# Input codes of a four-bit feed-forward: excess on ScalarE, total in place in PSUM, code difference on VectorE, product alone on GpSimd

## The chip, the cores and the metric

The kernel runs on one core of a Trainium2 chip. The metric is the device time in microseconds (us) of one execution. The engines are TensorE (PE), VectorE (DVE), ScalarE (ACT), GpSimd (POOL) and the DMA queues of SyncE (SP). They run side by side and meet at semaphores.

## The reference

Eight blocks in a row, each added to a residual stream x of shape (8, 512, 128): a selective scan, a feed-forward in four-bit codes, linear attention, the same feed-forward again, a forgetting attention, a linear map with signs, a rotary attention, and the linear map again. Only the two four-bit feed-forwards are touched, and in them only how the normalised input gets its codes:

```python
def _layernorm(x, axis=-1, eps=1e-05):
    m = jnp.mean(x, axis=axis, keepdims=True)
    v = jnp.var(x, axis=axis, keepdims=True)
    return (x - m) / jnp.sqrt(v + eps)

def fp4_quant_dequant(x):            # BLOCK = 16
    xb = x.reshape(shape[:-1] + (shape[-1] // BLOCK, BLOCK))
    scale = jnp.max(jnp.abs(xb), axis=-1, keepdims=True) / 6.0
    scale = jnp.maximum(scale, jnp.float32(1e-12))
    xn = xb / scale
    idx = jnp.searchsorted(_MID, jnp.abs(xn))
    q = _GRID[idx] * jnp.sign(xn) * scale
    return q.reshape(shape)

gate = fp4_linear(x, w_gate)         # fp4_linear: both operands through fp4_quant_dequant
y = fp4_linear(x, w_up)
h = jax.nn.silu(gate) * y
return fp4_linear(h, w_down)
```

The grid is 0, 0.5, 1, 1.5, 2, 3, 4, 6.

## The kernel before, in words

The kernel is a chain of stages. A stage opens its tiles and semaphores, writes out by hand what each engine does in order (one function per engine in a block), and ends with a barrier of all engines; nothing of the next stage starts before it. `ffn0_stages` holds two of them, `fx` (input codes) and `fh` (hidden layer), and is called twice, once for each four-bit feed-forward.

Stage `fx` works on 8 sequences of 512 tokens in PAIRS = 4 pairs. A pair is 8 tiles of 128 tokens by 128 channels, 1024 columns, in one of RING = 3 tiles of PSUM (`cps`, shown as fx_ps_c). Blocks of 16 channels lie next to each other, 64 blocks a pair.

- TensorE, `center(g)` (L728): 8 products with the centring matrix, 16 matmul instructions in the profile. g = 0 to 3 serves the moments and block maxima; g = 4 to 7 makes the same values again for the codes, since PSUM holds three pairs only. The last of them, center(7), writes the ring tile that pair 0 of the codes has used and so waits for it.
- ScalarE: squares with sums (L756), then logarithm and exponential for the inverse root (L772, L774).
- VectorE: block maxima (L787), the root's refinement (L794 to L801), then `codes` (L807 to L813) for all four pairs at once: normed, above (the scale, a hair larger), inv, both.
- Then for every pair k: VectorE `scaled` (L819) multiplies the tile in PSUM by both, so it holds xn. ScalarE `sizes` (L762) takes size = |xn| x 2^22. VectorE `total` takes mag = max(size, ROUND), ROUND = 1.5 x 2^22 (L824), and tot = mag + xn (L826): adding so large a number rounds xn to the grid. GpSimd takes q = tot - mag (L843) and xq = q x above (L846), 1024 columns each. TensorE `back` (L737) transposes the 8 tiles into two PSUM tiles, and ScalarE `out` (L767) copies them to XQ, which stage `fh` reads.

Most tiles behind the ring are double (index k % 2), and the waits on semaphores say when one is free again. The order on each engine is as written; VectorE goes scaled(0), then scaled(k+1), total(k).

Of the kernel before, what the change touches and what calls it, by code (L numbers as in the profile page):

```python
# [9 lines left out]
ALU = mybir.AluOpType  # L10
# [3 lines left out]
P = 128  # L14
# [6 lines left out]
FQ = 16  # L21
# [672 lines left out]
def ffn0_stages(nc, w, X):  # L694
# [7 lines left out]
    with Stage(nc, "ffn") as outer:  # L702
        XQ = outer.sb("xq", [P, B, T])
        with Stage(nc, "fx") as st:
# [8 lines left out]
            size, mag, tot, q, xq = ([st.sb(f"{n}{k}", [P, NB, FQ]) for k in range(2)] for n in ("size", "mag", "tot", "q", "xq"))  # L713
            s = st.sems("cent sq lnv rough var v1 v2 rstd amax normed above inv both xn size mag tot q xq back out")
            with st.block() as block:

                @block.tensor
                def _(pe):
                    def center(g):
                        k, before = g % PAIRS, g - RING  # L720
                        if before >= PAIRS:
                            pe.wait_ge(s.tot, before - PAIRS + 1)
                        elif before >= 0:
                            pe.wait_ge(s.sq, TOK * (before + 1))
                            pe.wait_ge(s.amax, before + 1)
# [22 lines left out]
                def _(act):  # L748
# [35 lines left out]
                def _(dve):  # L784
# [4 lines left out]
                    def tokens(t):  # L789
                        return t[:, :, :].rearrange("p k (t a) -> p (k t) a", t=TOK)  # L790
# [12 lines left out]
                    def codes():  # L803
                        r = widen(rstd[:, :, :].rearrange("p k t -> p (k t)"), XB)
                        dve.wait_ge(s.rstd, 1)
                        dve.wait_ge(s.amax, PAIRS)
                        dve.tensor_tensor(tokens(normed), tokens(amax), r, ALU.mult).then_inc(s.normed, 1)  # L807
                        dve.wait_ge(s.normed, 1)
                        dve.tensor_scalar(above[:, :, :], normed[:, :, :], ABOVE / 6.0, ABOVE * 1e-12, ALU.mult, ALU.max).then_inc(s.above, 1)
                        dve.wait_ge(s.above, 1)  # L810
                        dve.reciprocal(inv[:, :, :], above[:, :, :]).then_inc(s.inv, 1)
                        dve.wait_ge(s.inv, 1)
# [1600 lines left out]
```

## Time and profile before

| what | value |
|---|---|
| median of 3 runs | 2164.16 us (2164.16 to 2165.03) |
| the profiled execution | 2161.56 us |
| its span on the core | 2159.8 us |
| busy TensorE / VectorE / ScalarE / GpSimd | 85% / 78% / 65% / 49% |
| DMA | 39 GB/s mean |

The profile is of one execution; its times count from the span's start. A row of the order of time gives start, duration, engine, line, operation, the tiles out<-in, their sizes and a count; brackets hold the idle time of the engine ahead of it and what ended that. The granted TensorE clock is 1.00 for 2.4 GHz and 0.50 for 1.2 GHz. The two runs of stage `fx` begin near 381 and 629 us.

### The profile page before, as it was taken

Reading aid. Unit: us, or ns where it says so; the run is one execution under the profiler, and the core shown is the slowest. Engines: PE = TensorE matmul, PEld = TensorE weight load, DVE = VectorE, ACT = ScalarE, POOL = GpSimd, SP = SyncE. Lnnn points to the kernel's source line nnn. Section 1 sums busy time; section 2 is a strip of 40 time slices with the busy share of each in tenths; the row PEclk is TensorE's granted clock in tenths of the full one; section 3 lists DMA queues with packets and bytes.
Section 4 is the critical chain, followed back from the end, with each engine's and each line's share of the span. In section 5 each row is a group of like instructions: output and inputs, shape, how many; then the busy total and the mean of one; then the engine's idle time right before and its main releaser. Section 6 shows DMA issues by size and latency. Waiting matters only on the chain. (4 is left out here: it accounts for less than half of the span.)

```text
span 2159.8 us, 36543 instructions
## 1 busy us (share of the span) xinstructions
PE 1836.5 (85%) x12003; PEld 886.7 (41%) x12003; DVE 1680.9 (78%) x2274; ACT 1400.2 (65%) x2314; POOL 1056.2 (49%) x1121
## 2 busy tenths in 40 slices
PE   5558886687886857999999999999999967789997
PEld 2123332553664423555555555555554423222222
DVE  5979996596346958888888888888887636798884
ACT  3547774375335736777777777777776524689994
POOL 0167774364106714666666666666666521431112
PEclk9779998699997979999999999999999978999999
DMA  3000000000000011111111112221111100422210
GB/s 96 0 15 0 0 0 0 1 1 1 0 0 0 1 57 42 48 62 62 58 62 59 56 61 62 62 62 61 57 56 64 42 20 15 103 75 58 57 48 39
DMA packets 71432, 84.48 MB, mean 39 GB/s; under 512 B 20544, under 2 KB 44032, under 8 KB 71168
## 3 DMA queue, kind: packets, MB, share of 16 engines
q1 hardware_dynamic: 69536, 81.69, 12.5%
q8 instruction: 91, 1.49, 0.3%
q10 hardware_dynamic: 1728, 0.67, 0.1%
q14 instruction: 77, 0.63, 0.1%
HBM read 71.95 MB, written 9.57 MB: 38 GB/s over the span
## 5 line engine op out<-in xcount | busy, mean ns | idle before, releaser
L1761 DVE SCALAR_TENSOR_TENSOR fu_kv<-fu_ps_kv,fa_vec,fu_kv 128x511 f32<-128x511 f32 (+2 forms) x384 | 286.0, 746 | 56.3 <-ACT fu_kv L1633 51.1
L1844 POOL TENSOR_TENSOR fu_ds<-fu_p 128x768 f32<-128x768 f32 x64 | 115.8, 1810 | 188.7 <-PE fu_ps_ss L1532 188.5
L2199 ACT ACTIVATE rt_p<-rt_ps_s 128x1024 f32<-128x1024 f32 x192 | 185.6, 1029 | 25.1 <-PE rt_ps_s L2130 25.1
L1492 PE MATMUL fu_ps_s<-fu_qn,fu_kn 64*128 64x512 f32 (+3 forms) x1024 | 190.0, 468 | 1.4 <-DVE fu_sg L1722 0.7
L625 POOL TENSOR_TENSOR scan_hC<-scan_h,scan_c 128x1024 f32<-128x1024 f32 x64 | 150.9, 2357 | 71.7 <-DVE scan_h L601 71.7
L1633 ACT ACTIVATE fu_kv<-fu_ps_kv,fa_vec 128x512 f32<-128x512 f32 x128 | 88.4, 690 | 108.2 <-PE fu_ps_kv L1541 64.9
L1522 PE MATMUL fu_ps_n<-fu_p,fu_vt 128*64 128x512 f32 (+3 forms) x1024 | 151.9, 439 | 0.0
L601 DVE TENSOR_TENSOR_SCAN scan_h<-scan_dA,scan_ps_b 128x1024 f32<-128x1024 f32 x64 | 146.4, 2287 | 2.2
L524 PE MATMUL scan_ps_y<-scan_hC,w_ident 128*128 128x512 f32 x256 | 125.5, 612 | 26.5 <-POOL scan_hC L625 14.9
L2095 POOL TENSOR_SCALAR rt_d<-rt_d 128x1024 f32<-128x1024 f32 x32 | 35.0, 1094 | 184.0 <-DVE rt_d L2220 178.3
L1860 POOL TENSOR_TENSOR fu_kn<-fu_ks,fu_rb 128x512 f32<-128x512 f32 x64 | 81.5, 1274 | 68.8 <-DMA fu_rb<-rms_rows 68.7
L1637 ACT ACTIVATE fu_ps_kv<-fu_kv 128x512 f32<-128x512 f32 x128 | 77.2, 603 | 57.1 <-DVE fu_kv L1761 57.0
L1492 PEld LDWEIGHTS fu_ps_s<-fu_qn,fu_kn 64*128 64x128 f32 x1024 | 82.9, 185 | 73.8 <-issue 54.6
L2144 PE MATMUL rt_ps_o<-rt_p,rt_va 128*32 128x512 f32 x768 | 103.3, 610 | 7.0 <-ACT rt_p L2199 5.6
L571 ACT ACTIVATE scan_c<-scan_ps_c 128x1024 f32<-128x1024 f32 x64 | 65.6, 1024 | 67.2 <-PE scan_ps_c L545 48.2
L567 ACT ACTIVATE scan_dA<-ssm_delta,w_decay 128x511 f32 (+1 forms) x128 | 85.2, 717 | 13.2 <-DVE scan_dA L587 13.0
L1014 POOL TENSOR_TENSOR fh_q<-fh_tot,fh_mag 128x352 f32<-128x352 f32 x64 | 59.8, 934 | 63.4 <-DVE fh_tot L990 63.4
L2130 PE MATMUL rt_ps_s<-ra_stackq,ra_stackk 48*128 48x512 bf16 x512 | 84.5, 391 | 6.3 <-PEq L75 5.7
L1522 PEld LDWEIGHTS fu_ps_n<-fu_p,fu_vt 128*64 128x64 f32 x1024 | 63.4, 136 | 63.4 <-issue 60.2
L1864 POOL TENSOR_TENSOR fu_num<-fu_num,fu_sg 128x512 f32<-128x512 f32 x64 | 82.6, 1291 | 9.9 <-DVE fu_sg L1722 9.8
L1848 POOL TENSOR_TENSOR fu_ds<-fu_ds,fu_p 128x512 f32<-128x512 f32 x64 | 82.4, 1287 | 5.0
L1541 PE MATMUL fu_ps_kv<-w_XN,fa_wp 128*128 128x512 f32 x128 | 73.3, 655 | 12.3 <-PEq L75 8.9
(384 smaller groups left out, 5316.7 us busy)
## 6 DMA issues: line engine op xcount, KB each, us to landing
fu_rb<-rms_rows SPq DMA_DIRECT2D x256, 128.0 KB, 2.9
fu_ro<-rms_rows SPq DMA_DIRECT2D x128, 128.0 KB, 3.0
ra_stackq<-rope_parts SPq DMA_DIRECT2D x168, 32.0 KB
ra_stackk<-rope_parts SPq DMA_DIRECT2D x168, 32.0 KB
w_X<-in_xT SPq DMA_DIRECT2D x4, 512.0 KB, 7.3
fa_wp<-in_wp SPq DMA_DIRECT2D x8, 256.0 KB
fa_cr<-ncum_rows SPq DMA_DIRECT2D x128, 3.0 KB
rope_parts<-ra_hi SPq DMA_DIRECT2D x16, 128.0 KB, 2.5
```

What stands on the lines that cost most here:

```text
L524: i = pe.matmul(yps[:, :], w.ident[:, :], hC[p % (BEHIND + 2)][:, j, :], start=(p == 0 and j == 0), stop=False)
L567: m = act.activation(dA[p % 2][:, j, 1:T], DL[:, n, 1:T], ACT.Exp, scale=w.decay[:, k:k + 1])
L601: dve.tensor_tensor_scan(flat[0], flat[1], flat[2], 0.0, ALU.mult, ALU.add).then_inc(s.scan, 1)
L625: pool.tensor_tensor(hC[p % (BEHIND + 2)][:, :, :], hst[p % 2][:, :, :], csb[p % 2][:, :, :], ALU.mult).then_inc(s.hC, 1)
L1492: pe.matmul(sps[:, h, at:at + T - t * P], k[head(h), t * P:(t + 1) * P], q[head(h), t * P:T], start=(at == 0), stop=False)
L1522: m = pe.matmul(nps[head(h), t * P:T], VT[p % VR][:, t, head(h)], e[:, h, :], start=(t == 0), stop=(t == 2))
L1633: act.activation(KV[:, at, :], kvps[:, at, :], ACT.Copy, scale=vec[:, a % GA, last:last + 1]).then_inc(done, 1)
L1761: dve.scalar_tensor_tensor(acc, kvps[:, at, 0:T - j], vec[:, a % GA, w:w + 1], acc, ALU.mult, ALU.add).then_inc(done, 1)
L1844: pool.tensor_tensor(DS[:, :, :], P0[p % 2][:, :, P:T], P13[:, :, 0:3 * P], ALU.add).then_inc(s.d1, 1)
L2130: m = pe.matmul(sps[u % RING][:, e, :], stack[1][rows, pair, t * P:(t + 1) * P], stack[0][rows, pair, :], start=True, stop=True)
L2144: m = pe.matmul(ops[32 * j:32 * j + 32, :], va[n % 2][:, t, 4 * q4 + j, :], p[j // 2][:, j % 2, :], start=(t == 1), stop=(t == 0))
L2199: act.activation(p[:, :, :], sps[unit(g, t, i) % RING][:, :, :], ACT.Exp, scale=DH_B ** -0.5).then_inc(s.exp, 1)
```

## The change

Per pair, VectorE no longer makes mag and GpSimd no longer makes q. ScalarE follows size with over = Relu(size - ROUND), one more pass, so that mag = over + ROUND. VectorE's total becomes one instruction that writes (over + ROUND) + xn over xn in PSUM. A second VectorE instruction, minus_code, writes (over + ROUND) - total, which is the code with its sign turned, to SBUF. GpSimd only multiplies by above, in two halves of 512 columns, and `back` waits for each half. The copy to XQ turns the sign with scale=-1. The scale chain `codes` runs in two halves of two pairs: codes(0), scaled(0), scaled(1), codes(1). center(7) waits for minus_code(0) where it waited for total(0).

```diff
                         if before >= PAIRS:
-                            pe.wait_ge(s.tot, before - PAIRS + 1)
+                            pe.wait_ge(s.q, before - PAIRS + 1)
...
                     def back(k):
-                        pe.wait_ge(s.xq, k + 1)
                         for j in range(2):
+                            pe.wait_ge(s.xq, 2 * k + j + 1)
...
                     def sizes(k):
                         act.wait_ge(s.xn, k + 1)
-                        act.wait_ge(s.mag, max(k - 1, 0))
-                        act.wait_ge(s.tot, max(k - 1, 0))
+                        act.wait_ge(s.over, max(k - 1, 0))
                         act.activation(size[k % 2][:, :, :], cps[(PAIRS + k) % RING][:, :, :], ACT.Abs, scale=STEP).then_inc(s.size, 1)
+                        act.wait_ge(s.size, k + 1)
+                        act.wait_ge(s.q, max(k - 1, 0))
+                        act.activation(over[k % 2][:, :, :], size[k % 2][:, :, :], ACT.Relu, bias=w.below_round).then_inc(s.over, 1)
...
-                            act.activation(XQ[:, 2 * k + j, :], qps[j][:, :], ACT.Copy).then_inc(s.out, 1)
+                            act.activation(XQ[:, 2 * k + j, :], qps[j][:, :], ACT.Copy, scale=-1.0).then_inc(s.out, 1)
...
-                    def codes():
+                    def codes(half):
+                        pairs = slice(half * PAIRS // 2, (half + 1) * PAIRS // 2)
...
                     def total(k):
-                        dve.wait_ge(s.size, k + 1)
-                        dve.wait_ge(s.q, max(k - 1, 0))
-                        dve.tensor_scalar(mag[k % 2][:, :, :], size[k % 2][:, :, :], ROUND, None, ALU.max).then_inc(s.mag, 1)
-                        dve.wait_ge(s.mag, k + 1)
-                        dve.tensor_tensor(tot[k % 2][:, :, :], mag[k % 2][:, :, :], cps[(PAIRS + k) % RING][:, :, :], ALU.add).then_inc(s.tot, 1)
+                        xn = cps[(PAIRS + k) % RING][:, :, :]
+                        dve.wait_ge(s.over, k + 1)
+                        dve.scalar_tensor_tensor(xn, over[k % 2][:, :, :], ROUND, xn, ALU.add, ALU.add).then_inc(s.tot, 1)
+
+                    def minus_code(k):
+                        dve.wait_ge(s.tot, k + 1)
+                        dve.wait_ge(s.xq, max(2 * k - 2, 0))
+                        dve.scalar_tensor_tensor(q[k % 2][:, :, :], over[k % 2][:, :, :], ROUND, cps[(PAIRS + k) % RING][:, :, :], ALU.add, ALU.subtract).then_inc(s.q, 1)
...
-                    codes()
+                    codes(0)
                     scaled(0)
+                    scaled(1)
+                    codes(1)
                     for k in range(PAIRS):
-                        if k + 1 < PAIRS:
-                            scaled(k + 1)
                         total(k)
+                        if k + 2 < PAIRS:
+                            scaled(k + 2)
+                        minus_code(k)
...
-                        pool.tensor_tensor(q[k % 2][:, :, :], tot[k % 2][:, :, :], mag[k % 2][:, :, :], ALU.subtract).then_inc(s.q, 1)
                         pool.wait_ge(s.q, k + 1)
-                        pool.wait_ge(s.back, max(2 * k - 2, 0))
-                        pool.tensor_tensor(xq[k % 2][:, :, :], q[k % 2][:, :, :], widen(above[:, k, :], FQ), ALU.mult).then_inc(s.xq, 1)
+                        pool.wait_ge(s.above, 2 * k // PAIRS + 1)
+                        for j in range(2):
+                            pool.wait_ge(s.back, max(2 * k + j - 3, 0))
+                            blocks = slice(j * HALF, (j + 1) * HALF)
+                            pool.tensor_tensor(xq[k % 2][:, blocks, :], q[k % 2][:, blocks, :], widen(above[:, k, blocks], FQ), ALU.mult).then_inc(s.xq, 1)
```

On VectorE, from the first scaled of stage `fx` to its end, before:

```order
L819 TENSOR_TENSOR fx_ps_c<-fx_ps_c,fx_both 128x1024 x2
L824 TENSOR_SCALAR fx_mag<-fx_size 128x1024
L826 TENSOR_TENSOR fx_tot<-fx_mag,fx_ps_c 128x1024
L819 TENSOR_TENSOR fx_ps_c<-fx_ps_c,fx_both 128x1024
L824 TENSOR_SCALAR fx_mag<-fx_size 128x1024
L826 TENSOR_TENSOR fx_tot<-fx_mag,fx_ps_c 128x1024
L819 TENSOR_TENSOR fx_ps_c<-fx_ps_c,fx_both 128x1024
L824 TENSOR_SCALAR fx_mag<-fx_size 128x1024
L826 TENSOR_TENSOR fx_tot<-fx_mag,fx_ps_c 128x1024
```

The same stretch of VectorE now, from the second half of the scale chain on (its line numbers are those of the changed kernel; L822 is scaled, L827 total, L832 minus_code):

```order
L816 TENSOR_TENSOR fx_both<-fx_inv,fx_rstd 128x128
L827 SCALAR_TENSOR_TENSOR fx_ps_c<-fx_over,fx_ps_c 128x1024
L822 TENSOR_TENSOR fx_ps_c<-fx_ps_c,fx_both 128x1024
L832 SCALAR_TENSOR_TENSOR fx_q<-fx_over,fx_ps_c 128x1024
L827 SCALAR_TENSOR_TENSOR fx_ps_c<-fx_over,fx_ps_c 128x1024
L822 TENSOR_TENSOR fx_ps_c<-fx_ps_c,fx_both 128x1024
L832 SCALAR_TENSOR_TENSOR fx_q<-fx_over,fx_ps_c 128x1024
L827 SCALAR_TENSOR_TENSOR fx_ps_c<-fx_over,fx_ps_c 128x1024
L832 SCALAR_TENSOR_TENSOR fx_q<-fx_over,fx_ps_c 128x1024
```

The last scaled (pair 3) now stands behind total(1) and ahead of minus_code(1). Both scaled(0) and scaled(1) stand ahead of the second half of the chain.

On ScalarE, the end of the same stage, before:

```order
L774 ACTIVATE fx_rough<-fx_lnv 128x32
L762 ACTIVATE fx_size<-fx_ps_c 128x1024 x3
L767 ACTIVATE ffn_xq<-fx_ps_q 128x512 x2
L762 ACTIVATE fx_size<-fx_ps_c 128x1024
L767 ACTIVATE ffn_xq<-fx_ps_q 128x512 x6
```

And now (L761 is size, L764 the new excess, L769 the copy out):

```order
L776 ACTIVATE fx_rough<-fx_lnv 128x32
L761 ACTIVATE fx_size<-fx_ps_c 128x1024
L764 ACTIVATE fx_over<-fx_size,w_consts 128x1024
L761 ACTIVATE fx_size<-fx_ps_c 128x1024
L764 ACTIVATE fx_over<-fx_size,w_consts 128x1024
L761 ACTIVATE fx_size<-fx_ps_c 128x1024
L764 ACTIVATE fx_over<-fx_size,w_consts 128x1024
L769 ACTIVATE ffn_xq<-fx_ps_q 128x512 x2
L761 ACTIVATE fx_size<-fx_ps_c 128x1024
L764 ACTIVATE fx_over<-fx_size,w_consts 128x1024
L769 ACTIVATE ffn_xq<-fx_ps_q 128x512 x6
```

Each size is followed by its excess, and pair 3's two stand behind the copies out of pair 0. No table load has joined. The order on TensorE is unchanged.

## Rows read from the trace of the kernel before

**Rows 1.** Page: busy time, share of span, instructions of each engine.
```profile
PE 1836.5 (85%) x12003; PEld 886.7 (41%) x12003; DVE 1680.9 (78%) x2274; ACT 1400.2 (65%) x2314; POOL 1056.2 (49%) x1121
```
**Rows 2.** Order of time, first run of stage fx, to the next stage's first matmuls.
```profile
395.93 0.43 DVE L807 TENSOR_TENSOR fx_normed<-fx_amax,fx_rstd 128x256 f32<-128x256 f32 x1
...
396.72 1.75 DVE L811 RECIPROCAL fx_inv<-fx_above 128x256 f32<-128x256 f32 x1
...
398.96 2.36 DVE L819 TENSOR_TENSOR fx_ps_c<-fx_ps_c,fx_both 128x1024 f32<-128x1024 f32 x2
400.23 2.15 ACT L762 ACTIVATE fx_size<-fx_ps_c 128x1024 f32<-128x1024 f32 x2 [5.75 <-DVE fx_ps_c L819]
401.29 0.69 DVE L824 TENSOR_SCALAR fx_mag<-fx_size 128x1024 f32<-128x1024 f32 x1
...
403.29 3.58 PE L728 MATMUL fx_ps_c<-w_center,w_X 128*128 128x128 f32 x16 [5.99 <-DVE fx_tot L826]
403.32 2.35 POOL L843 TENSOR_TENSOR fx_q<-fx_tot,fx_mag 128x1024 f32<-128x1024 f32 x1 [45.77 <-DVE fx_tot L826]
404.29 1.93 DVE L824 TENSOR_SCALAR fx_mag<-fx_size 128x1024 f32<-128x1024 f32 x1
...
405.74 2.26 POOL L846 TENSOR_TENSOR fx_xq<-fx_q,fx_above 128x1024 f32<-128x1024 f32 x1
...
419.81 1.93 POOL L846 TENSOR_TENSOR fx_xq<-fx_q,fx_above 128x1024 f32<-128x1024 f32 x1
...
421.80 1.97 PE L737 MATMUL fx_ps_q<-w_ident,fx_xq 128*128 128x128 f32 x8 [2.34 <-POOL fx_xq L846]
422.95 0.60 ACT L767 ACTIVATE ffn_xq<-fx_ps_q 128x512 f32<-128x512 f32 x1 [2.86 <-PE fx_ps_q L737]
423.80 0.60 ACT L767 ACTIVATE ffn_xq<-fx_ps_q 128x512 f32<-128x512 f32 x1 [0.26 <-PE fx_ps_q L737]
...
425.30 2.69 PE L880 MATMUL fh_ps_g<-w_gate,ffn_xq 128*128 128x352 f32 x4 [1.53 <-PEq L75]
```
**Rows 3.** Order of time, second run of stage fx: its first and last.
```profile
642.81 0.42 DVE L807 TENSOR_TENSOR fx_normed<-fx_amax,fx_rstd 128x256 f32<-128x256 f32 x1
...
670.68 0.60 ACT L767 ACTIVATE ffn_xq<-fx_ps_q 128x512 f32<-128x512 f32 x1 [0.26 <-PE fx_ps_q L737]
```
**Rows 4.** Groups by line and shape: busy us, mean ns | idle before.
```profile
L476 DVE SCALAR_TENSOR_TENSOR ssmd_ps_t<-ssmd_ps_t,ssm_dx 128x1024 f32<-128x1024 f32 x4 | 4.9, 1225 | 0.0
L480 DVE SCALAR_TENSOR_TENSOR ssmd_neg<-ssmd_ps_t,ssm_dx 128x1024 f32<-128x1024 f32 x4 | 4.9, 1216 | 0.0
...
L1999 ACT ACTIVATE rp_ps_a<-rp_ln,w_consts 128x1024 f32<-128x1024 f32 x8 | 8.9, 1119 | 0.3
```
**Rows 5.** One line's instructions: ns min/median/max, first and last start us.
```profile
L826 DVE TENSOR_TENSOR fx_tot<-fx_mag,fx_ps_c x8: 1220/1222/1222, 402.0 to 660.1; 128x1024 f32<-128x1024 f32 x8
L1722 DVE SCALAR_TENSOR_TENSOR fu_sg<-fu_sg,fu_ps_s x64: 676/679/689, 898.7 to 1737.8; 128x512 f32<-128x512 f32 x64
L990 DVE SCALAR_TENSOR_TENSOR fh_tot<-fh_mag,fh_h x32: 877/1455/1471, 437.1 to 756.9; 128x704 f32<-128x704 f32 x32
L1017 POOL TENSOR_TENSOR fh_hq<-fh_q,fh_above x64: 786/788/1542, 439.1 to 761.6; 128x352 f32<-128x352 f32 x64
```
**Rows 6.** TensorE by stretch: length, busy (instructions), granted clock, DMA share, GB/s.
```profile
403.20:404.20 1.00, 0.91 (x4) 0.50 0.00 0
...
406.50:407.00 0.50, 0.37 (x3) 0.97 0.00 0
...
410.00:411.00 1.00, 0.00 (x0) 0.50 0.00 0
...
653.00:654.00 1.00, 0.95 (x5) 0.50 0.00 0
```
**Rows 7.** Order of time, start of the stage's centring after an idle stretch.
```profile
381.59 15.71 PE L728 MATMUL fx_ps_c<-w_center,w_X 128*128 128x128 f32 x112 [8.75 <-PEq L75]
385.38 0.28 ACT L756 ACTIVATE fx_sqr<-fx_ps_c 128x128 f32<-128x128 f32 x1 [2.55 <-PE fx_ps_c L728]
```

More of the change, by code:

```diff
@@ L712, in ffn0_stages @@
             amax, normed, above, inv, both = (st.sb(n, [P, PAIRS, NB]) for n in ("amax", "normed", "above", "inv", "both"))
-            size, mag, tot, q, xq = ([st.sb(f"{n}{k}", [P, NB, FQ]) for k in range(2)] for n in ("size", "mag", "tot", "q", "xq"))
-            s = st.sems("cent sq lnv rough var v1 v2 rstd amax normed above inv both xn size mag tot q xq back out")
+            size, over, q, xq = ([st.sb(f"{n}{k}", [P, NB, FQ]) for k in range(2)] for n in ("size", "over", "q", "xq"))
+            s = st.sems("cent sq lnv rough var v1 v2 rstd amax normed above inv both xn size over tot q xq back out")
             with st.block() as block:
@@ L787, in maxima, with tokens @@
                         dve.tensor_reduce(amax[:, k, :], cps[k % RING][:, :, :], AX_X, ALU.max, apply_absolute_value=True).then_inc(s.amax, 1)
-                    def tokens(t):
-                        return t[:, :, :].rearrange("p k (t a) -> p (k t) a", t=TOK)
+                    def tokens(t, pairs):
+                        return t[:, pairs, :].rearrange("p k (t a) -> p (k t) a", t=TOK)
                     def roots():
@@ L801, in roots @@
                         dve.scalar_tensor_tensor(rstd[:, :, :], v2[:, :, :], 1.5, rough[:, :, :], ALU.add, ALU.mult).then_inc(s.rstd, 1)
-                    def codes():
-                        r = widen(rstd[:, :, :].rearrange("p k t -> p (k t)"), XB)
+                    def codes(half):
+                        pairs = slice(half * PAIRS // 2, (half + 1) * PAIRS // 2)
+                        r = widen(rstd[:, pairs, :].rearrange("p k t -> p (k t)"), XB)
                         dve.wait_ge(s.rstd, 1)
                         dve.wait_ge(s.amax, PAIRS)
[L807 to L812, printed above, removed]
-                        dve.tensor_tensor(tokens(both), tokens(inv), r, ALU.mult).then_inc(s.both, 1)
+                        dve.tensor_tensor(tokens(normed, pairs), tokens(amax, pairs), r, ALU.mult).then_inc(s.normed, 1)
+                        dve.wait_ge(s.normed, half + 1)
+                        dve.tensor_scalar(above[:, pairs, :], normed[:, pairs, :], ABOVE / 6.0, ABOVE * 1e-12, ALU.mult, ALU.max).then_inc(s.above, 1)
+                        dve.wait_ge(s.above, half + 1)
+                        dve.reciprocal(inv[:, pairs, :], above[:, pairs, :]).then_inc(s.inv, 1)
+                        dve.wait_ge(s.inv, half + 1)
+                        dve.tensor_tensor(tokens(both, pairs), tokens(inv, pairs), r, ALU.mult).then_inc(s.both, 1)
                     def scaled(k):
                         xn = cps[(PAIRS + k) % RING][:, :, :]
-                        dve.wait_ge(s.both, 1)
+                        dve.wait_ge(s.both, 2 * k // PAIRS + 1)
                         dve.wait_ge(s.cent, PAIRS + k + 1)
@@ L830, in _ @@
                     roots()
[L831 removed]
+                    codes(0)
                     scaled(0)
+                    scaled(1)
+                    codes(1)
                     for k in range(PAIRS):
[L834 to L835 removed]
                         total(k)
+                        if k + 2 < PAIRS:
+                            scaled(k + 2)
+                        minus_code(k)
                 @block.gpsimd
                 def _(pool):
+                    HALF = NB // 2
                     for k in range(PAIRS):
[L841 to L843 removed]
                         pool.wait_ge(s.q, k + 1)
[L845 to L847 removed]
+                        pool.wait_ge(s.above, 2 * k // PAIRS + 1)
[3 more added lines that the diff above has]
+                            pool.tensor_tensor(xq[k % 2][:, blocks, :], q[k % 2][:, blocks, :], widen(above[:, k, blocks], FQ), ALU.mult).then_inc(s.xq, 1)
+                    pool.wait_ge(s.xq, 2 * PAIRS)
         with Stage(nc, "fh") as st:
```

3 lines of the change are left out of this document (removed).

## The prediction, made before the changed kernel ran

> **What bounds the kernel now.** I read the busy shares first. TensorE 85%, VectorE 78% [rows 1]: no engine is full, and the page's tenths change from stage to stage, so the whole-kernel shares say little about a change inside one stage. The change touches only the input-code stage (names fx_) of the four-bit feed-forward. It runs twice, with a barrier on both sides, so what it loses or gains goes into the span one for one. I then read the order of time of its first run [rows 2]. I count from the first scale operation, 395.93 (L807), to the end of the last ScalarE copy, 423.80 + 0.60 = 424.40: 28.47 us. In the second run [rows 3] the same two instructions stand at 642.81 and 670.68 + 0.60 = 671.28: 28.47 again. Both runs are priced alike.
>
> Inside that stretch the reader sees two things [rows 2]. First, GpSimd sets the pace: q takes 2.35 and the product 1.93 for each of four pairs, and they stand in a row with little between them from 403.32 to 419.81 + 1.93 = 421.74, 18.4 us of the 28.47. Second, VectorE and GpSimd block each other. The mag operation takes 0.69 alone (401.29), but 1.93 at 404.29, ending 406.22, half a microsecond after the q that began at 403.32 ended (405.67). The product at 405.74 takes 2.26 where the undisturbed one at 419.81 takes 1.93. The tot operation (L826), with one operand in PSUM, takes 1.22 in all eight cases, whatever GpSimd does [rows 5].
>
> **The change, part by part.** Prices, each for one instruction:
> - GpSimd: q (2.35) goes. The product becomes two halves of 512. From 0.79 at 352 columns [rows 5] and 1.93 at 1024 [rows 2] the slope is 1.70 ns a column, so a half is 0.79 + 160 x 1.70 ns = 1.06, and a pair 2.15.
> - VectorE: mag goes; tot becomes scalar_tensor_tensor in place in PSUM, and minus_code is new. Both have near twins of the same shape: L476 in place in PSUM 1.23, L480 PSUM to SBUF 1.22 [rows 4]. VectorE instructions that wait for nothing follow each other 0.09 before the end of the one ahead (L819 x2: 2.36 for two of 1.23) [rows 2].
> - ScalarE: Relu with a bias, 1024 columns out of SBUF. Its row is absent; the nearest is L1999, same shape with bias, 1.12 [rows 4]. Bounds: 1.02 (L762, without bias, out of PSUM; 2.15 for two with a gap between them) and 1.20 (twice the 0.60 of a 512-column copy) [rows 2]. I take 1.12. No table load joins (order on ScalarE), and scale=-1.0 on the copy out is in the same instruction: 0 to 0.05, taken as 0.
> - The scale chain is cut in two. The whole chain takes 395.93 to 398.96, 3.03, 1.75 of it the reciprocal of 256 columns [rows 2]. Bounds for a half are 1.5 (all in proportion) and 3.03 (none of it); a fixed part of about 0.1 to 0.2 in each of four instructions makes it about 1.87, near the lower end, since the reciprocal is long. The second half runs while ScalarE makes the first excess, so it is hidden, except that total 0 waits for it.
> - A new wait: the seventh centring (16 matmuls) now waits for q 0 instead of tot 0, and scaled(3) stands on VectorE ahead of minus_code(1), total(2) and all that follows. What the centring takes: sixteen matmuls after an idle stretch, 381.59 to the ScalarE instruction that waits for them at 385.38: 3.79 [rows 7]. Before, this centring started at 403.29 after 5.99 idle, at a granted clock of 0.50, the lower level, 1.2 GHz [rows 2, 6]. Bounds: half of 3.79, 1.9, if it ran at 2.4 GHz, and 3.8; I take 3.75, near the upper, since the idle time ahead of it only grows. total(1) covers 1.14 of the wait; the rest is bare.
> - PE's transposes start at half a product. At 0.50 four of them let ScalarE start 1.15 later (421.80 to 422.95) [rows 2].
>
> The walk, from the zero above; handovers 0.03 on one engine, 0.05 to ScalarE and TensorE, 0.08 to GpSimd (tot ends 403.24, TensorE starts 403.29, GpSimd 403.32) [rows 2, 5]:
> scaled(0) ends 3.10, scaled(1) 4.24, second chain 6.02. Sizes and excesses: 0 ready at 5.32, 1 at 7.5. total(0) 6.02 to 7.25; scaled(2) ends 8.39; minus_code(0) ends 9.53. So far little is won: before, q 0 ended at 9.74 (405.67). total(1) ends 10.67. The centring starts 9.58 and ends 13.33, so VectorE idles 2.7. scaled(3) ends 14.61, minus_code(1) 15.75, total(2) 16.89, minus_code(2) 18.15. For total(3), ScalarE: the transposes of pair 0 follow the centring on TensorE, copies out end 16.0, size(3) and excess(3) end 18.18. So total(3) runs 18.22 to 19.45 and minus_code(3) ends 20.71. GpSimd: products of pair 1 end 17.98, of pair 2 20.38, of pair 3 20.79 to 21.85 and to 22.94. The last four transposes and one copy: 0.06 + 1.15 + 0.60, end 24.75.
> 28.47 - 24.75 = 3.7 a stage, twice = 7.4 us. Against its own execution: span 2159.8, 2161.56 in all, gives 2154.2. The runs' median stands 2.6 above that profiled execution (2164.16); the same 7.4 off it gives 2156.7, my forecast.
>
> VectorE is what is late next: from 6.02 to 20.71 it does ten instructions, 12.0, and idles 2.7, with GpSimd's last product behind it. Sensitivities by the same walk: centring 3.4 instead of 3.75, 0.35 more per stage; halves of 1.18 (half of q's 2.35) instead of 1.06, 0.24 less; a Relu of 1.20 instead of 1.12, 0.1 less; a centring at the full clock, 1.9 instead of 3.75, 1.8 more. Together they bound a stage's gain between 3.3 and 5.6.
>
> One rule speaks against the move. mag costs VectorE 0.69 alone, while ScalarE's pass costs 1.12 [rows 2, 4]. The Trainium skill (ScalarE: Activation LUTs, Rules for kernel authors) says that relu, max and add belong on VectorE, not on ScalarE, since VectorE is faster per element. By the walk the dearer pass is hidden for pairs 0 to 2 and costs 0.16 for pair 3. By that rule all four would show, which is the third rival's sum.
>
> **Rivals.**
> 1. The clock joins in. In the new tail TensorE's transposes stand closer together than before, when the next stage's first four matmuls still took 2.69 [rows 2]. If the clock goes to 2.4 GHz there, the last transposes gain 0.5, and the next stage's first eight matmuls, twice 2.69 = 5.4, would take half of it and gain 2.0 to 2.7, together 2.5 a stage. For: in the first run the clock rose 3.2 us into the centring. Against: it had not yet in the second, and by 410, when the transposes of pair 0 were over, it was back at 0.50 [rows 6]. Time: 2156.7 - 5.0 = 2151.7. Chance 0.13.
> 2. VectorE and GpSimd exclude each other for the new forms too, so the side flips. The feed-forward's scalar_tensor_tensor with both operands in SBUF (L990) takes 0.88 at best and 1.46 in the median, with GpSimd at work beside it [rows 5]. If one SBUF operand were enough, the end would run strictly in turn: total(2), half, minus_code(2), half, total(3), half, minus_code(3), three halves: four turns of about 1.0 added, end 28.81. That is 0.34 later than before per stage, 2164.16 + 0.7 = 2164.8, slower than before; it decides from the fourth such turn. Against: tot's 1.22, and L1722, a scalar_tensor_tensor with one operand in PSUM, takes 676 to 689 ns in all 64 [rows 5]. The Trainium skill (SBUF — State Buffer, Who interferes with whom) excludes it as well: at most one SBUF input, no contention. Chance 0.05.
> 3. ScalarE is on the path throughout: the dearer pass, 1.12 - 0.69 = 0.43 for four pairs, 1.7 a stage, gives back 3.4 of 7.4: 2160.1. For: excess(3) is already 0.16 late in the walk, and it hangs on the centring and the copies ahead of it. Against: the excesses of pairs 0 to 2 are ready 0.7, 1.9 and 5 us before VectorE comes to them. Chance 0.12.
> 4. The change moves work and no time: the centring's wait and its followers cost what the q pass cost, 2164. For: q 0 ends only 0.2 earlier, and VectorE's new idle time is 2.7. Against: GpSimd's row of 18.4 falls to eight halves, 8.5. Chance 0.04.
>
> **How the numbers follow.** A measurement of this kernel tells from no change about 0.2%, 4.3 us. Forecast 0.66, with its own range 2154 to 2159; then rivals 1 to 4 as above. The clock of later stages can shift either way when they begin 4 and 7 us sooner; the profiled execution is itself 2.6 away from the median, so I allow 2.5. The range takes in rival 1 and rival 3: 2151.5 to 2161. Faster by over 4.3 (below 2159.8): forecast and rival 1, 0.79. Within: rivals 3 and 4 and half of rival 2, 0.17. Slower by more: the rest of rival 2 and a clock that turns out badly later, 0.04.
>
> **What would show it.** L810 to the last copy: 24.7 in both runs. GpSimd: eight products of 1.06, none stretched. VectorE: 1.22 for both new forms, one idle of 2.5 to 2.8 ahead of the fourth L822, released by TensorE. ScalarE's Relu 1.12. Wrong would be: a new form above 1.3 beside GpSimd; the Relu above 1.2; a centring of 2.1 at the full clock (then the end is near 22.9); or a stage 3.7 shorter with a span that is not, which would put the loss into the stages behind it.

## The result, and the profile after

The changed kernel takes 2145.83 us in the median of 5 runs (2143.77 to 2152.60), the kernel before 2164.16 (2162.28 to 2165.03): ratio 0.9931, interval 0.9909 to 0.9952. The forecast was 2156.7 with a range down to 2151.5. The sign was right; the gain, 18 us by the medians and 15 by the ratio, is at least twice the 7.4 forecast. Profiled executions: 2161.56 before, 2144.47 after, 17.1 apart. Runs that something on the chip disturbed are left out of every median and range below: 2178.77 us with scaled(3) later, 2770.28 with 30 spare matmuls, and 6242.99 of the kernel before.

The page's first part, engines' busy time, share, instructions:

```profile
PE 1825.6 (85%) x12003; PEld 879.1 (41%) x12003; DVE 1681.9 (78%) x2282; ACT 1409.1 (66%) x2322; POOL 1034.4 (48%) x1121
```

Against [rows 1], GpSimd lost 22 us and ScalarE gained 9. TensorE has the same 12003 instructions and 11 us less in them, though none of its instructions was moved; it is a first hint of the clock.

The changed kernel's groups by line and shape, columns as in [rows 4]:

```profile
L856 POOL TENSOR_TENSOR fx_xq<-fx_q,fx_above 128x512 f32<-128x512 f32 x16 | 16.6, 1058 | 87.1 <-DVE fx_q L832 87.1
...
L827 DVE SCALAR_TENSOR_TENSOR fx_ps_c<-fx_over,fx_ps_c 128x1024 f32<-128x1024 f32 x8 | 9.8, 1224 | 0.0
L832 DVE SCALAR_TENSOR_TENSOR fx_q<-fx_over,fx_ps_c 128x1024 f32<-128x1024 f32 x8 | 9.7, 1216 | 0.1
```

These prices came out: a half product 1.058 us (priced 1.06), both new VectorE forms 1.22, none stretched beside GpSimd. The order of time, first run of the stage:

```profile
396.00 0.29 DVE L810 TENSOR_TENSOR fx_normed<-fx_amax,fx_rstd 128x128 f32<-128x128 f32 x1
...
401.95 1.22 DVE L827 SCALAR_TENSOR_TENSOR fx_ps_c<-fx_over,fx_ps_c 128x1024 f32<-128x1024 f32 x1
...
405.48 3.78 PE L728 MATMUL fx_ps_c<-w_center,w_X 128*128 128x128 f32 x16 [8.11 <-DVE fx_q L832]
...
409.37 1.23 DVE L822 TENSOR_TENSOR fx_ps_c<-fx_ps_c,fx_both 128x1024 f32<-128x1024 f32 x1 [2.80 <-PE fx_ps_c L728]
410.93 1.03 ACT L761 ACTIVATE fx_size<-fx_ps_c 128x1024 f32<-128x1024 f32 x1
411.99 1.15 ACT L764 ACTIVATE fx_over<-fx_size,w_consts 128x1024 f32<-128x1024 f32 x1
414.03 1.22 DVE L827 SCALAR_TENSOR_TENSOR fx_ps_c<-fx_over,fx_ps_c 128x1024 f32<-128x1024 f32 x1
415.29 1.22 DVE L832 SCALAR_TENSOR_TENSOR fx_q<-fx_over,fx_ps_c 128x1024 f32<-128x1024 f32 x1
416.59 2.07 POOL L856 TENSOR_TENSOR fx_xq<-fx_q,fx_above 128x512 f32<-128x512 f32 x2 [0.32 <-DVE fx_q L832]
418.72 0.66 PE L737 MATMUL fx_ps_q<-w_ident,fx_xq 128*128 128x128 f32 x4 [0.36 <-POOL fx_xq L856]
419.41 0.60 ACT L769 ACTIVATE ffn_xq<-fx_ps_q 128x512 f32<-128x512 f32 x1 [0.42 <-PE fx_ps_q L737]
420.91 1.42 PE L890 MATMUL fh_ps_g<-w_gate,ffn_xq 128*128 128x352 f32 x4 [1.53 <-PEq L75]
```

And the second run, to VectorE's first product h of the next stage (fh_h):

```profile
635.66 0.29 DVE L810 TENSOR_TENSOR fx_normed<-fx_amax,fx_rstd 128x128 f32<-128x128 f32 x1
...
659.17 0.60 ACT L769 ACTIVATE ffn_xq<-fx_ps_q 128x512 f32<-128x512 f32 x1 [0.19 <-PE fx_ps_q L737]
660.67 1.42 PE L890 MATMUL fh_ps_g<-w_gate,ffn_xq 128*128 128x352 f32 x4 [1.54 <-PEq L75]
663.38 0.89 DVE L978 TENSOR_TENSOR fh_h<-fh_gt,fh_ps_u 128x704 f32<-128x704 f32 x1 [7.33 <-PE fh_ps_u L896]
```

The same product before:

```profile
430.43 0.89 DVE L968 TENSOR_TENSOR fh_h<-fh_gt,fh_ps_u 128x704 f32<-128x704 f32 x1 [15.97 <-PE fh_ps_u L886]
...
676.87 0.89 DVE L968 TENSOR_TENSOR fh_h<-fh_gt,fh_ps_u 128x704 f32<-128x704 f32 x1 [15.53 <-PE fh_ps_u L886]
```

The stage runs 396.00 to 420.01, 24.01, and 635.66 to 659.77, 24.11, against 28.47 twice [rows 2, 3]. The time from the last copy of fx to the first fh_h, called the next start from here on, shrinks too. The 17.1 us can be laid out by how much earlier the same instruction comes:

| stretch | before | after | gain |
|---|---|---|---|
| stage fx, both runs | 28.47, 28.47 | 24.01, 24.11 | 8.8 |
| next start, both | 6.03, 5.59 | 3.60, 3.61 | 4.4 |
| everything else | | | 3.9 |

The second row goes with the clock: the first four matmuls of fh take 1.42 instead of 2.69 [rows 2], and the experiments below test it. TensorE by stretch of the changed kernel, columns as in [rows 6]:

```profile
414.00:415.00 1.00, 1.00 (x4) 0.50 0.00 0
416.00:417.00 1.00, 1.00 (x6) 0.79 0.00 0
420.00:421.00 1.00, 0.09 (x1) 1.00 0.00 0
```

The granted clock rises in the tail of fx, where transposes now stand close, and is still 1.00 (2.4 GHz) when fh starts. In the third row most of the 3.9 lies in code that is the same in both. The forgetting attention (names fu_) starts 13.73 earlier (801.39 to 787.66), the sign-map stage sf 14.57 (1752.01 to 1737.44), the normalisation behind it 16.69 (1783.74 to 1767.05). The sf stage alone is 2.1 shorter. Its start before:

```profile
1752.00:1755.00 3.00, 2.99 (x5) 0.50 0.01 3
1755.00:1758.00 3.00, 3.00 (x5) 0.50 0.00 0
```

and after:

```profile
1737.50:1740.50 3.00, 3.00 (x5) 0.50 0.00 0
1740.50:1743.50 3.00, 3.00 (x8) 0.95 0.00 0
```

The same matmuls, six microseconds at 0.50 before and about three after. So three questions: was the 7.4 a right sum for right reasons; is the 4.4 really the clock; and does the 3.9 belong to the change?

### The profile page after: what moved, and what is told of

It is laid out like the page before. It is cut to its first block and busy times, and to the rows that moved or that the text cites. A ratio compares the mean times of both kernels' runs of the same rounds, so it can differ in the third digit from the quotient of the medians.

```text
span 2142.7 us, 36569 instructions
## 1 busy us (share of the span) xinstructions
PE 1825.6 (85%) x12003; PEld 879.1 (41%) x12003; DVE 1681.9 (78%) x2282; ACT 1409.1 (66%) x2322; POOL 1034.4 (48%) x1121
## 5 line engine op out<-in xcount | busy, mean ns | idle before, releaser
L571 ACT ACTIVATE scan_c<-scan_ps_c 128x1024 f32<-128x1024 f32 x64 | 65.5, 1024 | 67.2 <-PE scan_ps_c L545 48.1
L1874 POOL TENSOR_TENSOR fu_num<-fu_num,fu_sg 128x512 f32<-128x512 f32 x64 | 82.5, 1289 | 10.2 <-DVE fu_sg L1732 10.1
```

## The experiments

In all of them a "spare" matmul is one of 128x128 by 128 columns whose result nothing reads. Ratios are to the kernel before on the same chip, in brackets the interval; they are no quotients of the two medians, and the two can differ by 1 to 4 us. Every experiment has one profile, and its stage lengths and next starts are those of that one execution.

### The terms of the sum

**Product whole.** The changed kernel with one product of 1024 columns a pair.

```diff
...
-                        for j in range(2):
-                            pool.wait_ge(s.back, max(2 * k + j - 3, 0))
-                            blocks = slice(j * HALF, (j + 1) * HALF)
-                            pool.tensor_tensor(xq[k % 2][:, blocks, :], q[k % 2][:, blocks, :], ...)
+                        pool.wait_ge(s.back, max(2 * k - 2, 0))
+                        pool.tensor_tensor(xq[k % 2][:, :, :], q[k % 2][:, :, :], ...)
```

> The changed kernel with the product in one instruction of 1024 columns and one wait, as before. Theory: the stage ends 1.1 to 1.4 later (a second half of 1.0 ahead of the last transposes, and eight of them in a row instead of four), the clock at the next stage's start is as in the changed kernel: 2145.8 + 2.5 = 2148.3. Rival (the halves are what keeps TensorE busy enough): the next stage starts at 0.50, 4.6 more, 2153.

Measured: 2146.93, 0.9933 [0.9917, 0.9949]; stage 25.16 and 25.11; next start 3.59 and 3.61. The halves are worth 1.1 a stage in the profile. For the two stages that is 2.2 us, less than the scatter of the whole time (2143.44 to 2155.65), so the medians can't show it.

**Halves alone.** The kernel before with only its product in halves.

> The kernel before with only the product in two halves and a wait for each. Theory: GpSimd still carries q, so only the tail gains: the last transposes and the copy behind half a product, 0.8 of 2.66, less 0.15 of fixed cost a pair: 0.2 to 0.5 a stage, 2163.2 against 2163.6; the clock at the next stage's start stays at 0.50, since the gaps between transposes stay. Rival (the halves make the transposes close enough to raise the clock): 4 less, 2159.

Measured: 2160.59, 0.9991 [0.9981, 1.0001]; stage 28.19 and 28.21, 0.27 shorter; next start 6.03 and 5.72, at the lower clock. With q still on GpSimd the halves bring a quarter of what they bring in the changed kernel. So the halves are not the gain by themselves; they shorten the tail once q and mag are taken away.

**Scale chain whole.** The changed kernel with codes() for four pairs at once.

```diff
-                        pairs = slice(half * PAIRS // 2, (half + 1) * PAIRS // 2)
+                        pairs = slice(0, PAIRS)
...
                     scaled(1)
-                    codes(1)
```

> The changed kernel with the scale chain whole again (all four pairs at once, ahead of scaled(0)). Theory: scaled(0) starts 1.15 later and the second chain of 1.9 goes from VectorE; then total(0) waits for excess 0, which is ready at 6.5 instead of 5.3, so the end moves by 0.5 later a stage: 2146.8. Rival (the split is worth its 1.15): 2.3 in all, 2148.1.

Measured: 2150.09, 0.9953 [0.9938, 0.9967]; stage 25.04 and 25.06, so the cut is worth 1.0 a stage, nearer the rival's 1.15 than my 0.5. Of the 4.4 a stage, 1.1 goes when the halves are undone and 1.0 when the cut is; the other 2.3 I put down to the moved work, which no run tests by itself.

### The centring between

**scaled(3) later.** The fourth scaling stands behind minus_code(1) and total(2), and ScalarE makes all sizes before it copies. VectorE's order, with its loop written out:

```diff
                     total(1)
-                    scaled(3)
                     minus_code(1)
                     total(2)
+                    scaled(3)
                     minus_code(2)
```

> The changed kernel with scaled(3) moved behind minus_code(1) and total(2), and all sizes ahead of the copies out on ScalarE. Theory (the centring wait costs VectorE 2.7 idle a stage, since scaled(3) blocks what is ready behind it): the idle time ahead of scaled(3) falls to under 0.5 and the stage ends 1.2 to 1.4 earlier, 2.6 in all, 2143.2. Rival (the fourth pair's own chain from the centring on sets the end: scaled, size, excess, total, minus code, product): the end moves by less than 0.4 a stage.

Measured: 2143.64 (2141.64 to 2146.34), 0.9912 [0.9898, 0.9927]; stage 23.18 and 23.17. In order of time:

```profile
407.56 1.23 DVE L821 TENSOR_TENSOR fx_ps_c<-fx_ps_c,fx_both 128x1024 f32<-128x1024 f32 x1 [0.41 <-PE fx_ps_c L728]
411.07 1.23 DVE L826 SCALAR_TENSOR_TENSOR fx_ps_c<-fx_over,fx_ps_c 128x1024 f32<-128x1024 f32 x1 [1.16 <-ACT fx_over L764]
```

VectorE's idle time of 2.80 shrinks to 0.41, but 1.16 of it comes back as a wait of total(3) for ScalarE's excess; the stage is 0.8 and 0.9 shorter. Next start 5.29 and 5.30, with fh's first four matmuls at 2.49. The tail of fx reached the upper clock here too, but the clock fell 0.2 us into fh, behind the same 1.5 us of TensorE's idle time that it outlasted in the changed kernel. TensorE by stretch:

```profile
417.00:418.00 1.00, 0.00 (x0) 1.00 0.00 0
418.00:419.00 1.00, 0.72 (x2) 0.74 0.00 0
418.50:419.50 1.00, 1.00 (x3) 0.50 0.07 16
```

So leaving fx at the upper clock is not enough; it has to last into fh.

**The same, one step.** Only minus_code(1) ahead of scaled(3).

> The changed kernel with minus_code(1) ahead of scaled(3) on VectorE and nothing else moved. Theory (pair 1's code is ready to be made while VectorE waits for the centring, so it costs nothing there): minus_code(1) fills 1.2 of the 2.8 idle, all behind scaled(3) comes 1.1 earlier, but excess(3) on ScalarE stays at 18.2 of the stage and now sets total(3): the end moves by 0.1 to 0.4 a stage, 2145.3. Rival (VectorE alone sets the end): 1.1 a stage, 2143.6.

Measured: 2147.23, 0.9935 [0.9922, 0.9948]; stage 23.81 twice, 0.2 to 0.3 shorter. The wait before scaled(3) is 1.55, that of total(3) for its excess 0.38; next start 5.05 and 5.06, lower clock.

**64 spare matmuls ahead of center(7)**, so that the centring finds a high clock.

```diff
                         center(g)
+                    for i in range(64):
+                        pe.matmul(qps[1][:, 0:P], X[:, i % B, 0:P], w.center[:, :], start=True, stop=True)
```

> The changed kernel with 64 spare matmuls (into a tile that is free until the first transposes) in TensorE's 8.1 us of idle time ahead of the seventh centring, so that it comes to it at the full clock. Theory (the centring is at 1.2 GHz only because TensorE idles before it, and it is on the path): it takes 2.0 instead of 3.8, VectorE's idle time ahead of scaled(3) falls from 2.8 to 1.1, and the stage ends 1.7 earlier, 22.3; 3.4 in all, 2142.4. Rival (something else than the centring lets scaled(3) go): the idle time and the end stay.

Measured: 2156.94 (2151.34 to 2162.72), 0.9980 [0.9968, 0.9991]; stage 28.50 and 28.55.

```profile
397.18 14.46 PE L743 MATMUL fx_ps_q<-w_center,w_X 128*128 128x128 f32 x128
411.48 1.95 PE L728 MATMUL fx_ps_c<-w_center,w_X 128*128 128x128 f32 x16
413.53 1.23 DVE L824 TENSOR_TENSOR fx_ps_c<-fx_ps_c,fx_both 128x1024 f32<-128x1024 f32 x1 [7.00 <-PE fx_ps_c L728]
```

The clock did what was wanted: 1.95 for sixteen matmuls instead of 3.78. But one spare is two instructions in the profile, so 64 took 14.46 and held the centring back by 6; I had mis-sized the dose. The stage is as long as before the change, and yet the next start is 3.60 and 3.61, at the upper clock.

**30 spare matmuls** in the same place.

> The changed kernel with 30 spare matmuls (60 instructions in the profile, some 6.9 us) ahead of the seventh centring, mended from the run with 64, which took 14.5 us and held the centring back. There the centring itself took 1.95 at the full clock. Theory (the centring's 3.8 is on the path): it starts at 9.6 of the stage and takes 2.0, VectorE's idle time ahead of scaled(3) is 1.0, the stage ends at 22.3 instead of 24.0; with the next stages' clock as in the changed kernel, 3.4 in all, 2142.4. Rival (the stage's end is set elsewhere): 24.0.

Measured: 2144.87 (2144.54 to 2149.34), 0.9927 [0.9914, 0.9940]; stage 22.73 and 22.61.

```profile
397.21 6.86 PE L743 MATMUL fx_ps_q<-w_center,w_X 128*128 128x128 f32 x60
405.48 2.05 PE L728 MATMUL fx_ps_c<-w_center,w_X 128*128 128x128 f32 x16 [1.41 <-DVE fx_q L834]
407.64 1.23 DVE L824 TENSOR_TENSOR fx_ps_c<-fx_ps_c,fx_both 128x1024 f32<-128x1024 f32 x1 [1.07 <-PE fx_ps_c L728]
```

The centring's 1.73 less comes out as 1.73 less idle time of VectorE, and as a stage 1.3 and 1.5 shorter. The prediction gave a full-clock centring 1.8 a stage. The next start was at the lower clock in the first run (5.57) and the upper in the second (3.60).

### Is the 4.4 the clock?

**Spare matmuls in the tail of the kernel before**: no part of the change, only TensorE kept busy between its last transposes.

```diff
                         back(k)
+                        if k:
+                            pe.wait_ge(s.tot, 2)
+                            spare(2, (10, 10, 2)[k - 1])
```

> The kernel before, with spare matmuls (10, 10 and 2, into a free tile of PSUM) behind the transposes of pairs 1, 2 and 3 of the input-code stage, so that TensorE is busy to the stage's end; nothing else is changed. Theory (half of the unforeseen gain is TensorE's clock at the start of the hidden-layer stage): the granted clock reaches 1.00 before the stage ends, the first four matmuls of the next stage take 1.42 instead of 2.69 and its first product stands 2.7 instead of 5.1 and 4.7 after them; 2.3 a stage, 4.6 in all, near 2159.5, stage fx itself at most 0.5 shorter than 28.47. Rival (the next stage starts faster because it starts earlier): nothing happens, 2164.

Measured: 2154.06 (2151.33 to 2157.51) against 2162.69, 0.9966 [0.9953, 0.9979]; stage 27.65 and 27.68; next start 3.61 twice. In order of time:

```profile
424.85 1.42 PE L888 MATMUL fh_ps_g<-w_gate,ffn_xq 128*128 128x352 f32 x4 [1.14 <-PEq L75]
```

Work that nothing uses makes the kernel before faster, by 8.6 us by the medians and 7.4 by the ratio. In the profile, 9.1 faster, 1.6 of it is in fx, 4.4 in the next start, which has the same 3.6 as in the changed kernel, and 3.1 in other stages. So the clock alone, without any of the change, gives the second row of the table. The changed kernel run once more (below) gives the other half of the proof: the same program has 6.03 where the clock stays at the lower level and 3.60 where it is at the upper.

**The changed kernel, its gain in fx given back.** Four repeated reciprocals lengthen the first half of the scale chain; the tail stays as it is.

```diff
+                        for extra in range(0 if half else 4):
+                            dve.wait_ge(s.inv, extra + 1)
+                            dve.reciprocal(inv[:, pairs, :], above[:, pairs, :]).then_inc(s.inv, 1)
```

> The changed kernel with four repeats of the reciprocal in the first half of the scale chain (0.98 each with its gap, 3.9 a stage), so stage fx is about as long as before but ends as the changed one does. Theory (the close transposes at the end raise the clock): the next stage still starts at 1.00, and the time is the changed kernel's plus 7.9: 2145.8 + 7.9 = 2153.7. Rival (the length of the stage sets it): the first matmuls are slow again, 4.6 more, 2158.3. Later stages may shift by up to 3 either way.

Measured: 2157.35 (2149.93 to 2161.02, 11 runs), 0.9968 [0.9957, 0.9979]; stage 28.15 and 28.42; next start 5.86 and 6.03.

```profile
424.64 2.69 PE L893 MATMUL fh_ps_g<-w_gate,ffn_xq 128*128 128x352 f32 x4 [1.53 <-PEq L75]
```

I had expected the tail, whose instructions stand as close as in the changed kernel, to bring the clock again. In the profiled execution it didn't: the same tail, some 4 us later, left fx at 0.50 both times. But that execution, 2160.97, is one of the two slowest of the eleven and only 0.6 faster than the profiled one of before. It can't show where the gain of the median lies, 5 us by the medians and 7 by the ratio (in the profile, 0.4 in the stage and nothing in the next start). The four slowest executions have a mean granted clock of 0.941 to 0.944 and the seven faster ones, down to 2149.93, of 0.946 to 0.949. So the faster ones may well have had the clock at the start of fh; no trace of them shows it.

**The same with spares in TensorE's gaps** of the tail (9, 1, 1 and 6).

> The kernel with the 3.9 us of delay a stage, as run before (its profile showed the next stage's start at 0.50, its runs spread over 11 us), with spare matmuls in the gaps behind the transposes so that TensorE is busy to the stage's end. Theory (the changed kernel's gain beyond the stage is the clock at the hidden-layer stage's start, and whether it rises there depends on where the busy stretch falls): stage length as in the delayed kernel within 0.5, the next stage's first four matmuls at 1.42, first product 3.6 after the last copy instead of 5.9 and 6.0; the median 4 to 5 below the delayed kernel's 2157.35, near 2153, with less spread. Rival (the start of the next stage is fast for another reason than the clock): no change against 2157.

Measured: 2162.04, 0.9978 [0.9961, 0.9995], in two groups, five runs at 2151.05 to 2152.53 and seven at 2161.72 to 2163.31; stage 27.95 and 27.96. The clock is 1.00 throughout the tail, and fh's first four matmuls take 1.42:

```profile
425.84 1.42 PE L904 MATMUL fh_ps_g<-w_gate,ffn_xq 128*128 128x352 f32 x4 [0.95 <-PEq L75]
```

Next start 4.36, since the last spares hold the barrier by 0.8. By the medians nothing is gained, by the ratio 4.8. The profile is of the upper group and loses 4.9 us at the start of the forgetting attention, code that no edit touches. That a program falls in two groups 10 us apart makes its median unfit to price a microsecond; the next three runs ask about that.

### Does the 3.9 belong to the change?

**The changed kernel once more**, without any edit.

> The changed kernel once more, unchanged, on the chip of the three others. Theory (9 us of spread are the granted clock at the starts of stages, which the runs do not have alike): again 2144 to 2153 with a median near 2146. Rival (the first median was luck of five runs): a median at 2150 or above.

Measured: 2147.42 (2143.50 to 2150.76), 0.9937 [0.9924, 0.9950]. The clock of the same program wasn't the same. In order of time (the first row has only the first two of the four matmuls, which took 2.69 together):

```profile
420.91 1.51 PE L890 MATMUL fh_ps_g<-w_gate,ffn_xq 128*128 128x352 f32 x2 [1.53 <-PEq L75]
...
660.28 1.42 PE L890 MATMUL fh_ps_g<-w_gate,ffn_xq 128*128 128x352 f32 x4 [1.54 <-PEq L75]
```

The first run of fx (24.46) leaves at the lower clock this time (next start 6.03), the second (24.37) at the upper (3.60). In the tail TensorE was as busy as in the first profile, and the clock stayed down. The same three microseconds, first profile and this one:

```profile
414.00:417.00 3.00, 2.73 (x12) 0.60 0.00 0
```
```profile
414.00:417.00 3.00, 2.72 (x11) 0.50 0.00 0
```

The profiled execution, 2144.11, came out as short as the first one all the same: here 10.1 of its 17.5 less than the profiled one of before lie in the first two rows of the table and 7.4 elsewhere.

**A pause of 13.4 us**, four reciprocals of 512 columns, in the normalisation ahead of the forgetting attention, on top of the change, with TensorE waiting: everything behind it stands where it stood before the change, nearly.

```diff
+                pe.wait_ge(s.idle, len(pauses))
...
+                for i, cols in enumerate(pauses):
+                    dve.wait_ge(s.idle, i)
+                    dve.reciprocal(fine[0][:, 0:cols], src[:, 0, 0:cols]).then_inc(s.idle, 1)
```

> The changed kernel with a pause of 13.4 us (four reciprocals of 512 columns at 3.3, TensorE waiting for them) at the start of the layer norm behind the second feed-forward, so that all later stages begin at the same times as in the kernel before. Theory (the part of the gain behind the feed-forwards, some 4 us in the forgetting attention and the last norm stages, is where TensorE's clock falls and rises against work that begins 13.5 us sooner): with the old times the old clock comes back: 2146.6 + 13.4 + 4 = 2164, and the stage at 1752 has its six cold microseconds again. Rival (the changed kernel leaves the later stages better for another reason): 2146.6 + 13.4 = 2160.

Measured: 2166.82 (2160.42 to 2169.20, 11 runs), 1.0018 [1.0009, 1.0026]. The changed kernel's two medians have the mean 2146.6; with 13.4 that is 2160, and 6.8 more went. Its fx, the same code as the changed kernel's, took 24.46 and 24.35, with next starts of 6.03 and 3.61, at the lower and the upper clock. Against the profile of before the forgetting attention's first scores stand 4.5 later (855.22 to 850.68) and sf 6.7. Sf starts at 1758.72 and is at the lower clock for two stretches of three:

```profile
1759.00:1762.00 3.00, 3.00 (x6) 0.50 0.00 0
1762.00:1765.00 3.00, 3.00 (x5) 0.51 0.00 0
```

**A pause of 1.75 us in the kernel before** (256 columns), same place.

> The kernel before with one pause of 1.75 us at the same place, nothing else. Theory (a shift alone re-times the clock in later stages): the time moves by something else than 1.75, by 1 to 4 us, either way; 2162.3 + 1.75 = 2164.1 is what a pure shift gives. Rival (later stages do not depend on when they begin): 2164.1 within 0.7.

Measured: 2168.21 (2162.19 to 2169.28, 11 runs), 1.0021 [1.0011, 1.0032]: 6.1 over before's 2162.07 by the medians, 4.5 by the ratio, for a pause of 1.75. Where the two profiles part, here the forgetting attention's first scores (L1492 before at 850.68):

```profile
857.89 1.13 PE L1497 MATMUL fu_ps_s<-fu_qn,fu_kn 64*128 64x512 f32 x4
```

7.2 later, when the stage began 4.0 later (805.43 to 801.39). The stretch from its first matmul to these scores is a clean measure, since all sixteen profiles run the same code in it: ten take 49.28 to 49.36, four 52.43 to 52.55 (the reciprocals in fx, scaled(3) later, both pauses), two 54.1 (spares with delay, and the last experiment below). Nothing lies between. The lengths go with the clock. The ten shortest have it at the lower level for 11.1 to 11.3 us of the stretch, the four of 52.5 for 13.6 to 18.2, the two of 54.1 for 18.6 and 21.9. Here are the same 3 us of the stretch, 45.6 from its start, before and with the pause of 1.75:

```profile
847.00:850.00 3.00, 3.00 (x18) 1.00 0.61 163
```
```profile
851.00:854.00 3.00, 2.31 (x10) 0.50 0.43 137
```

That four profiles with 13.6 to 18.2 have one length, and why the clock falls at one place or another, stays open. A stage can thus take another time though its code is the same, and a gain of a few microseconds in one stage is not the gain of the whole kernel.

### A version that beats both

Order of the one-step experiment, 30 spares ahead of center(7), and 3, 3 and 4 spares in the tail.

```diff
+                    for i in range(30):
+                        pe.matmul(qps[1][:, 0:P], X[:, i % B, 0:P], w.center[:, :], start=True, stop=True)
...
+                        if k:
+                            pe.wait_ge(s.q, 2)
+                            spare(cps[2][:, 0:XB, :].rearrange("p a q -> p (a q)"), (3, 3, 4)[k - 1])
```

> Both: 30 spare matmuls ahead of the centring, minus_code(1) ahead of scaled(3), and a few spare matmuls (3, 3, 4) behind the transposes of pairs 1 to 3 to hold the clock to the next stage. Theory: centring ends at 11.6, copies of pair 0 end at 13.4, excess(3) at 15.7, total(3) and minus_code(3) end at 18.2, last product 20.3, stage end 21.3 to 21.6: 2.5 a stage less than the changed kernel, 5 in all, 2140.8, and the next stage always starts at 1.00. Rival (the spare matmuls delay transposes or the barrier by as much): 23 to 24 a stage.

Measured: 2141.47 (2139.70 to 2148.62, four runs), 0.9903 [0.9889, 0.9918]; stage 21.23 twice.

```profile
405.80 2.05 PE L728 MATMUL fx_ps_c<-w_center,w_X 128*128 128x128 f32 x16 [1.41 <-DVE fx_q L842]
...
416.96 0.60 ACT L779 ACTIVATE ffn_xq<-fx_ps_q 128x512 f32<-128x512 f32 x1 [0.42 <-PE fx_ps_q L737]
418.77 1.42 PE L905 MATMUL fh_ps_g<-w_gate,ffn_xq 128*128 128x352 f32 x4 [0.95 <-PEq L75]
```

The stage is 2.8 and 2.9 shorter than the changed kernel's, 5.7 in all; next start 3.92, at the upper clock. Its interval lies below that of the changed kernel's series on the same chip (0.9924 to 0.9950), and overlaps a little with its first (0.9909 to 0.9952). The profile holds the long form, 54.1, of the stretch named above and is the slowest of its runs.

## Why the prediction was wrong

**The walk through fx held.** Counted from 396.00, the steps came at (forecast in brackets): total(0) begins at 5.95 (6.02), the centring at 9.48 (9.58), scaled(3) at 13.37 (13.33) after 2.80 of idle time (2.7), total(3) at 18.03 (18.22), minus_code(3) ends at 20.51 (20.71), GpSimd at 22.66 (22.94), the last copy at 24.01 (24.75). One term off the path came a microsecond earlier, ScalarE's last excess at 17.14 (18.18). The 7.4 measured 8.8 in one profile and 8.1 in the other. Of the 0.74 too much in the first run, 0.28 had gathered up to GpSimd's end; the rest is the last four transposes, 0.66 instead of 1.15 [rows 2], at the higher clock.

**The step that failed is the clock,** carried as rival 1 with a chance of 0.13. Its price was nearly right: 2.5 a stage forecast, 2.4 and 2.0 measured for the next start, plus 0.5 and 0.2 in the last transposes. Its chance wasn't: the forecast put the term at nothing. The profile's 17.1 are the 7.4 of the sum, 0.7 that the rest of the walk gave too little, 5.1 of the clock in and behind fx, and 3.9 elsewhere. Rival 1 by itself, 2151.7, lay inside the range; only together with the 3.9, the next step, does the time lie below it. My counter-argument was two places where the clock had not risen in the centring or had not stayed up behind it [rows 6]. But that is one busy stretch followed by idle time. In the new tail TensorE has transposes for two pairs a few microseconds apart, and is busy for 2.7 of the 3.0 us from 414 to 417. I had worked out in the walk that the tail closes up and did not follow TensorE's own busy time through it. That would have told me that the clock may rise, not that it will: the same 2.7 of 3.0 us are in the first fx of the second profile, at 0.50. The changed kernel's two profiles, and the one with the pause of 13.4, whose fx is the same code, start fh at the upper clock in four of six cases. Neither the order nor the length of the stage settles it. With the same tail and a stage of 28 us, the clock was at the lower level behind the reciprocals and at the upper behind 64 spares, twice each. What settles it in a given execution stays open.

**"I allow 2.5" for later stages was mis-sized.** About 4 us came from stages that are word for word the same. The pauses of 1.75 and 13.4 us cost 4.4 and 6.8 us beyond the pause, by the medians. So I take the last 4 us for no property of the four-bit codes; another shift could have taken them away. In sf it is the clock (six microseconds at 0.50 or three), and not its start alone: behind the reciprocals in fx it starts at 1753.65, 1.6 later than before, and takes 29.6 instead of 31.7. In the forgetting attention it is the stretch of 49.3, 52.5 or 54.1, which is longer in the profiles where the clock stays longer at the lower level; what chooses that stays open. It does not enter the result itself (49.29 before, 49.33 after).

**The other rivals.** Rival 2 fell: 1.22 for both new forms, in the mean of eight each, beside GpSimd or not. Rival 3 fell as a sum: ScalarE's pass took 1.15, and it shows on the path only when the centring's wait has gone (1.16 with scaled(3) late). The Trainium skill (ScalarE: Activation LUTs, Rules for kernel authors) puts max and relu on VectorE rather than on ScalarE. This trace doesn't bear that out as a cost of the move: VectorE's mag took 0.69 for pair 0 alone, and 1.93, 2.35 and 1.16 for the others, beside GpSimd at work. Rival 4 fell with GpSimd's 8.5 us in place of 18.4. The cut scale chain, which I valued at 0.5 when it was tried by itself, is worth 1.0.

## What to carry to other kernels

When a change closes TensorE's gaps ahead of a stage that starts with matmuls, follow TensorE's busy time through the new tail as carefully as the critical path, and price the next stage's start at both clocks. The same tail brought either level here, from one execution to another, so give the upper one a real chance and no certainty. Where it came, it was worth 2.0 to 2.4 us a time, half as much as the change gave in fx. A chain of instruction durations read from nearest twins gives a stage within a few per cent, but the whole-kernel time adds several microseconds of either sign from stages that are only shifted, so a range must hold them. To price a part of a change, read its stage in the profile; to prove a clock effect, add work that nothing reads.

## What the runs showed of the hardware that was not expected

- Twenty-two spare matmuls in each run of fx made the kernel before 7 to 9 us faster.
- One stretch of unchanged code has three lengths in sixteen profiles, 49.3, 52.5 and 54.1 us, and nothing between, with 11.1 to 11.3, 13.6 to 18.2, and 18.6 to 21.9 us of it at the lower clock.
- The same program reached fh's start at the upper clock in one profile and at the lower in another, after a tail in which TensorE was as busy. The Trainium skill (TensorE: Matmul & The Clock Gate, What's actually happening) says that the number of matmuls at the lower clock varies from run to run of one kernel; the two profiles of the changed kernel agree (next start 3.60 and 6.03 at the same place).
- A pause of 1.75 us cost 6.1, one of 13.4 cost about 20; 3.2 of the excess is that stretch.
- VectorE's forms with one operand in PSUM were never stretched beside GpSimd (1.22 before and after); it was mag, with its input and its output in SBUF, that had grown from 0.69 to 1.93 and 2.35.
